# Cross attention with quantised operands: heads in the outer loop, two token tiles in the inner, values applied to 256 columns at once

## The chip, the cores and the metric

One core of one Trainium2 chip runs the whole kernel. The metric is the device time of one execution in microseconds (us), lower being better. TensorE (PE in the profile), VectorE (DVE), ScalarE (ACT) and GpSimd (POOL) each run their own list of instructions in order, and wait for one another on semaphores; SyncE (SP) issues the loads and stores.

## What is computed

A decoder of two layers over two sequences of 256 tokens (512 tokens of width 256): attention, cross attention and a feed-forward part in each layer, each followed by adding the input and a normalisation over the 256 features. The change lies in the cross attention of the second layer, cut here to what matters:

```python
q = (x @ Wq + bq).reshape(1, B * N, H, hd)
kv = (cond @ Wkv + bkv).reshape(1, -1, 2, H, hd)
...
q = _fq_sym(q, axis=-1)
k = _fq_sym(k, axis=-1)
v = _fq_sym(v, axis=2)
attn = jnp.einsum('bhqd,bhkd->bhqk', q, k)
attn = jax.nn.softmax(attn.astype(jnp.float32), axis=-1)
attn = _fq_unsigned(attn, axis=-1)
out = jnp.einsum('bhqk,bhkd->bhqd', attn, v)
out = jnp.transpose(out, (0, 2, 1, 3)).reshape(B, N, C)
return out @ Wp + bp
```

There are 16 heads of 16 features, 512 queries and 1024 keys. `_fq_sym` rounds to whole steps of the largest magnitude divided by 127, `_fq_unsigned` to 255 steps. The kernel takes exp(score - maximum + log 255) and converts it to int16, which is the rounded probability before the division by the sum.

## The kernel before, in words

The program is six stages, each ended by its residual addition and normalisation; stage 5 is the one above. Its 512 queries are four token tiles of 128 (TT = 4), and a **unit** is one head of one token tile: 64 units, numbered u = 16 i + h (tile i outside, head h inside). A unit passes over four engines:

- PE multiplies the queries of the unit with all keys, two products of 512 columns into two banks of PSUM (`scores`, line 927).
- DVE adds the zero, writes the scores to SBUF in `sx` and takes their maximum per row (`maximum`, line 1390; the profile calls it CUSTOM_DVE_ANT_0). POOL turns the maximum into a bias (line 442).
- ACT takes the exponential of `sx` into `px` as int16, with the sum of each row (line 562).
- PE turns the 1024 columns, eight transposes of 128 columns through `ident_b` (`turn`, line 936), into bank 4 or 5.
- DVE or ACT copies that bank to `pTx` and casts it (`evacuate`, line 1399, or `evac_px`, line 580). Which one is set by `SHARE`: of every seven units ACT takes numbers 1, 3 and 5 (27 of 64), DVE the other four (37).
- PE multiplies the turned probabilities with the values, eight products of 128 columns with 32 columns of weights (`apply`, line 947), into bank 6 or 7.

The order of the work is written out by hand. In step u PE issues scores(u + 3), turn(u), apply(u - 1). DVE issues maximum(u + 2) and evacuate(u). ACT issues exp(u) and evac_px(u - 1). Scores have two pairs of banks, `sx` and `px` three buffers each, `pTx` two.

Each token tile is closed while the units of the next one run: ACT takes the 256 columns of sums out of PSUM (`evac_sums`, line 589), DVE inverts the sums of rows (line 1403), PE turns them (`turn_z`, line 955), ACT copies them (line 595), PE spreads them over the features (`spread_z`, line 961), DVE multiplies (`normalise`, line 1408), PE projects (`project`, through the helper of line 630), DVE adds the residual (`add`, line 1413) and takes the statistics (lines 1130 and 1131), POOL the inverse deviation (lines 391 and 392), and DVE scales (line 1136). The fourth tile has no units behind it, so these steps run one after another at the stage's end. PE then transposes the result for stage 6 (line 690).

## Time and profile before

| | |
|---|---|
| time of three executions | 565.52 us median (565.0 to 566.82) |
| span of the profiled execution | 564.0 us, 7942 instructions; the three executions above have no span shown, and what lies around this span is not shown apart |
| PE | 501.8 us busy, 89% of the span |
| DVE | 347.0 us busy, 62% |
| ACT | 232.3 us busy, 41% |
| POOL | 111.9 us busy, 20% |
| stage 5, first maximum to last product | 329.8 to 441.9 us |
| chain of work that ended last | PE 71%, DVE 18%, ACT 5% |

The shares are means over six stages of different kinds. PE's busy time counts matmuls that overlap in the engine's pipeline, so it says little about how much room PE has; the starts of its instructions say more.

### The profile page before, as it was taken

The page shows a single profiled execution, that of the slowest core. Times are in us where ns is not written, and L with a number is a line of the kernel's source. Part 1 is how long each engine was busy: PE and PEld are TensorE (multiplying, and loading weights), DVE is VectorE, ACT ScalarE, POOL GpSimd, SP SyncE. Part 2 cuts the span into 40 slices and gives each one's busy share as a digit, 9 for nine tenths or more (in the row PEclk, how much of TensorE's full clock was granted, in tenths as well). Part 3 has the DMA queues.
Part 4 walks back from the last instruction along what each step waited for, and adds up shares of the span by engine and source line. Part 5 has one row for each costly group of instructions (what it writes and reads, how often), then busy time and mean ns, then how long its engine had stood idle before and what let it go on. Part 6 is the DMA issues. An engine that isn't in the chain of part 4 may idle for free.

```text
span 564.0 us, 7942 instructions
## 1 busy us (share of the span) xinstructions
PE 501.8 (89%) x2848; PEld 321.1 (57%) x2879; DVE 347.0 (62%) x845; ACT 232.3 (41%) x546; POOL 111.9 (20%) x209
## 2 busy tenths in 40 slices
PE   4696979999979999999997389999998788999994
PEld 2264556666645567776676246676666545455552
DVE  2996367454556766666654679999999373121224
ACT  3331321222223764445541169999898420010100
POOL 8695033232333000000002501111111000000002
PEclk9987988999988999999999759999999889999998
DMA  8900000000000000000000060000000400000001
GB/s 309 309 20 1 1 0 1 1 2 0 1 0 0 2 1 1 2 1 1 1 1 0 0 273 28 2 2 2 2 2 2 150 0 0 0 1 0 0 1 37
DMA packets 9671, 16.32 MB, mean 29 GB/s; under 512 B 1305, under 2 KB 8281, under 8 KB 9305
## 3 DMA queue, kind: packets, MB, share of 16 engines
q1 hardware_dynamic: 9632, 15.82, 8.4%
q8 instruction: 23, 0.38, 0.3%
q14 instruction: 16, 0.12, 0.1%
HBM read 15.29 MB, written 0.52 MB: 28 GB/s over the span
## 4 chain that ended last, share of the span: by engine, by line
PE 71%; DVE 18%; ACT 5%; issue 4%; DMA 1%; POOL 1%; SPq 0%; POOLq 0%; DVEq 0%; ACTq 0%
PE ps L630 16%; PE ps L848 8%; PE ps L816 8%; PE ps L1033 5%; PE ps L780 5%; PE ps L947 4%; PE ps L829 4%; PE ps L927 4%; PE ps L744 4%; PE ps L936 4%; PE ps L751 3%; ACT area_b L562 2%; DVE area_a L1390 2%; PE ps L721 1%; DVE stats L1130 1%
## 5 line engine op out<-in xcount | busy, mean ns | idle before, releaser
L1390 DVE CUSTOM_DVE_ANT_0 area_a<-ps,zero,small 128x1024 f32<-128x1024 f32 x64 | 80.0, 1272 | 1.3 <-PE ps L927 1.3
L562 ACT ACTIVATE area_b<-area_a,small 128x1024 int16<-128x1024 f32 x64 | 72.9, 1142 | 5.9 <-POOL small L442 5.7
L391 POOL TENSOR_SCALAR var_eps<-meanvar 128x1 f32<-128x1 f32 x24 | 6.0, 252 | 288.0 <-DVE meanvar L1131 287.5
L630 PE MATMUL ps<-xT_odd,area_a 128*128 128x512 f32 x128 | 59.4, 609 | 0.0
L816 PE MATMUL ps<-area_a,area_b 128*128 128x512 f32 x96 | 49.4, 625 | 0.3 <-DVE area_a L1267 0.2
L1472 DVE TENSOR_TENSOR area_b<-ps,area_b 128x512 f32<-128x512 f32 x16 | 11.0, 688 | 59.3 <-ACT area_b L606 59.3
L848 PE MATMUL ps<-area_b,area_a 128*32 128x128 f32 x384 | 47.4, 275 | 0.0
L606 ACT ACTIVATE area_b<-ps 128x512 f32<-128x512 f32 x16 | 9.6, 597 | 84.6 <-PE ps L630 84.6
L936 PEld LDWEIGHTS ps<-ident_b,area_b 128*128 128x128 bf16 x512 | 34.0, 99 | 17.4 <-ACT area_b L562 5.3
L927 PE MATMUL ps<-area_b 128*128 128x512 bf16 x107 | 35.8, 404 | 7.5 <-DVE small L1390 3.5
L848 PEld LDWEIGHTS ps<-area_b,area_a 128*32 128x32 f32 x384 | 39.1, 110 | 5.7 <-issue 5.3
L947 PE MATMUL ps<-area_a,area_b 128*32 128x128 bf16 x512 | 40.0, 221 | 1.0 <-ACT area_a L580 0.8
L936 PE MATMUL ps<-ident_b,area_b 128*128 128x128 bf16 x512 | 40.0, 222 | 0.8 <-ACT area_b L562 0.7
L543 ACT ACTIVATE area_a<-area_b,small 128x128 f32<-128x128 f32 (+1 forms) x64 | 28.3, 443 | 28.8 <-DVE small L1279 28.8
L543 ACT ACTIVATE area_a<-area_a,small 128x128 f32<-128x128 f32 (+1 forms) x64 | 28.3, 443 | 27.9 <-DVE small L1279 27.9
L630 PEld LDWEIGHTS ps<-xT_odd,area_a 128*128 128x128 f32 x128 | 25.1, 197 | 25.3 <-issue 24.6
L947 PEld LDWEIGHTS ps<-area_a,area_b 128*32 128x32 bf16 x512 | 28.9, 97 | 9.0 <-issue 1.7
L829 PEld LDWEIGHTS ps<-ident,area_a 128*128 128x128 f32 x192 | 22.7, 141 | 18.1 <-issue 14.3
L442 POOL TENSOR_SCALAR small<-small 128x1 f32<-128x1 f32 x64 | 12.4, 194 | 101.9 <-DVE small L1390 101.9
L1033 PE MATMUL ps<-area_a,area_b 128*128 128x256 f32 x128 | 31.6, 391 | 0.9 <-DVE area_b L1477 0.9
L1279 DVE CUSTOM_DVE_ANT_0 area_a<-ps,window 128x128 f32<-128x128 f32 (+1 forms) x64 | 19.1, 354 | 21.0 <-PE ps L816 21.0
L519 ACT ACTIVATE area_a<-ps 128x512 f32<-128x512 f32 x16 | 9.6, 597 | 53.6 <-PE ps L751 53.6
(259 smaller groups left out, 896.5 us busy)
## 6 DMA issues: line engine op xcount, KB each, us to landing
area_a<-in_w_up_dram SPq DMA_DIRECT2D x1, 4096.0 KB, 13.6
area_a<-in_w_down_dram SPq DMA_DIRECT2D x1, 2048.0 KB, 8.2
area_b<-in_idx_row_dram SPq DMA_DIRECT2D x1, 1024.0 KB, 7.2
ctxT<-in_ctxT_dram SPq DMA_DIRECT2D x1, 1024.0 KB, 9.2
ctx_tok<-in_ctx_dram SPq DMA_DIRECT2D x1, 1024.0 KB, 12.8
w_qkv<-in_w_qkv_dram SPq DMA_DIRECT2D x1, 768.0 KB, 5.9
xT_even<-in_xT_dram SPq DMA_DIRECT2D x1, 512.0 KB, 3.9
wkvx<-in_wkvx_dram SPq DMA_DIRECT2D x1, 512.0 KB, 10.0
```

Source lines behind the costliest of these rows:

```text
L543: a = act.activation(unit_p1(u)[:, j, 0:nk, :], s1[u % 2][:, j, 0:nk * P].rearrange("p (b k) -> p b k", b=nk), ACT.Exp, bias=nmx1[:, u % 2 ...
L562: act.activation(px[:, u % PX, :], sx[:, u % 3, :], ACT.Exp, bias=nbx[:, u:u + 1], accum_out=zx[:, i, h:h + 1]).then_inc(sem("px_ready"), 1)
L630: mm = pe.matmul(dst, lhsT(c), rhs(c), start=start and c == 0, stop=stop and c == DC - 1, **kw)
L780: mm = pe.matmul(proj(i), prod[:, j % 2, i * P:(i + 1) * P], row_hot[:, j, :], start=False, stop=j == SJ - 1, skip_group_check=True)
L816: mm = pe.matmul(dst, qT1[:, g8, i * P:(i + 1) * P], kT1[:, g8 // UC, :, kt * P:(kt + 1) * P], start=True, stop=True)
L829: mm = pe.transpose(bank(4, 2)[:, at:at + P], unit_p1(u)[:, j, b, :], ident[:])
L848: mm = pe.matmul(dst, v1[:, (kt * (H1 // HU) + g8) * HU + j, :], unit_pT1(u)[:, j, b, :], start=j == 0 and b == 0, stop=j == HU - 1 and b ...
L927: mm = pe.matmul(bank(2 * (u % 2) + half), qTx[:, h // 2, h % 2, i * P:(i + 1) * P], kTx[:, h // 2, half * 512:(half + 1) * 512], start=Tr ...
L936: mm = pe.transpose(bank(4 + u % 2).bitcast(BF16)[:, k * P:(k + 1) * P], px[:, u % PX, k * P:(k + 1) * P].bitcast(BF16), ident_b[:])
L947: mm = pe.matmul(dst, ivh[:, k * HX + h, :], pTx[:, u % 2, k * P:(k + 1) * P], start=h % 2 == 0 and k == 0, stop=h % 2 == 1 and k == KT - 1)
L1033: mm = pe.matmul(proj(i), hidden[:, g % 2, i * P:(i + 1) * P], w_down[:, g, :], start=g == 0 and i % 2 == 0, stop=g == NG - 1, skip_group_ ...
L1390: dve.tensor_tensor_reduce(sx[:, u % 3, :], bank(2 * (u % 2), 2), zero[:].broadcast_to([P, B * M]), qsc[:, u // HX, u % HX:u % HX + 1], LO ...
```

## The change

Units are numbered anew: u = 32 b + 2 h + t, where b is a half (two token tiles), h the head and t the tile in the half. Two neighbouring units share a head, and the values are applied to both in one product of 256 columns. Division, projection and the steps around them are done once per half, 256 tokens wide, of which the residual, the statistics and the scaling stay per tile. The `SHARE` table, the depth of all queues and the number of score, maximum, exponential and evacuation instructions stay. One of the two `pTx` buffers moves to another area, and each holds 8 pieces of 256 columns, so an evacuation writes 8 pieces of 128 columns at a distance of 256.

```diff
-        rzTx = sb("rzTx", [HX, P])
-        attTx = sb("attTx", [P, 2, DC, P])
+        rzTx = sb("rzTx", [HX, 2 * P])
+        attTx = sb("attTx", [P, DC, 2 * P])
...
-        pTx = carve("a", DC * E1 * 2 * HE + 3 * B * M, [2, KT * P], BF16)
+        pTx = [carve("a", DC * E1 * 2 * HE + 3 * B * M, [KT, 2 * P], BF16), carve("b", 26 * N, [KT, 2 * P], BF16)]
...
+        def unit5(u):
+
+            b, rest = divmod(u, 2 * HX)
+            return b, rest // 2, rest % 2
...
             def evac_px(u):
                 act.wait_ge(sem("pTx_ps"), u + 1)
-                if u >= 2:
-                    act.wait_ge(sem("ox_ps"), u - 1)
-
-                act.activation(pTx[:, u % 2, :], bank(4 + u % 2).bitcast(I16), ACT.Copy).then_inc(sem("pTx_act"), 1)
...
+                if u >= 4:
+                    act.wait_ge(sem("ox_ps"), u // 2 - 1)
+
+                act.activation(pTx[u // 2 % 2][:, :, u % 2 * P:(u % 2 + 1) * P], bank(4 + u % 2).bitcast(I16).rearrange("p (k q) -> p k q", q=P),
+                               ACT.Copy).then_inc(sem("pTx_act"), 1)
...
-                def apply(u):
-
-                    i, h = divmod(u, HX)
-                    pTx_ready(pe, u)
+                def apply(m):
+
+                    b, h, _ = unit5(2 * m)
+                    pTx_ready(pe, 2 * m)
+                    pTx_ready(pe, 2 * m + 1)
                     c, pair = divmod(h // 2, P // PAIR)
-                    dst = bank(6 + i % 2)[pair * PAIR:(pair + 1) * PAIR, c * P:(c + 1) * P]
+                    dst = bank(6 + b)[pair * PAIR:(pair + 1) * PAIR, 2 * c * P:2 * (c + 1) * P]
                     for k in range(KT):
-                        mm = pe.matmul(dst, ivh[:, k * HX + h, :], pTx[:, u % 2, k * P:(k + 1) * P],
+                        mm = pe.matmul(dst, ivh[:, k * HX + h, :], pTx[m % 2][:, k, :],
                                        start=h % 2 == 0 and k == 0, stop=h % 2 == 1 and k == KT - 1)
                     mm.then_inc(sem("ox_ps"), 1)
...
+                def project(b):
+                    pe.wait_ge(sem("attx_ready"), b + 1)
+                    for t in range(2):
+                        dense(bank(6 + b)[:, t * D:(t + 1) * D], lambda c: attTx[:, c, t * P:(t + 1) * P],
+                              lambda c: wpx[:, c, :]).then_inc(sem("proj5"), 1)
...
-                    if u > HX and u % HX == 3:
-                        turn_z(u // HX - 1)
-                    if u > HX and u % HX == 5:
-                        spread_z(u // HX - 1)
-                    if u > HX and u % HX == 7:
-                        project(u // HX - 1)
-                    if u % HX == 1 and u > 2 * HX:
-
-                        pe.wait_ge(sem("res5_ready"), u // HX - 1)
-                    if u:
-                        apply(u - 1)
-                turn_z(TT - 1)
-                spread_z(TT - 1)
-                project(TT - 1)
+                    if u == 2 * HX + 3:
+                        turn_z(0)
+                    if u == 2 * HX + 5:
+                        spread_z(0)
+                    if u == 2 * HX + 7:
+                        project(0)
+                    if u and u % 2 == 0:
+                        apply(u // 2 - 1)
+                turn_z(1)
+                spread_z(1)
+                project(1)
...
                 def add(i):
-                    dve.wait_ge(sem("proj5"), i + 1)
+                    dve.wait_ge(sem("proj5"), 2 * (i // 2) + 2)
...
-                invert_z(TT - 1)
-                normalise(TT - 1)
-                add(TT - 1)
-                norm_stats(5, TT - 1)
-                norm_scale(5, TT - 1)
+                    at = u - 2 * HX
+                    if at == 1:
+                        invert_z(0)
+                    if at == 6:
+                        normalise(0)
+                    if at in (8, 10):
+                        add(at // 2 - 4)
+                        norm_stats(5, at // 2 - 4)
+                    if at == NORM_AT:
+                        norm_scale(5, 0)
+                    if at == NORM_AT + 2:
+                        norm_scale(5, 1)
+                invert_z(1)
+                normalise(1)
+                for i in range(2, TT):
+                    add(i)
+                    norm_stats(5, i)
+                for i in range(2, TT):
+                    norm_scale(5, i)
```

Where the order moves, in three places. First PE between two steps of the plain stretch, before (line 927 is scores, 936 turn, 947 apply):

```order
L927 MATMUL ps<-area_b 128x512 x2
L936 MATMUL ps<-ident_b,area_b 128x128 x8
L947 MATMUL ps<-area_a,area_b 32x128 x8
L927 MATMUL ps<-area_b 128x512 x2
L936 MATMUL ps<-ident_b,area_b 128x128 x8
L947 MATMUL ps<-area_a,area_b 32x128 x8
```

And with the change (line 935 is scores, 944 turn, 956 apply):

```order
L935 MATMUL ps<-area_b 128x512 x2
L944 MATMUL ps<-ident_b,area_b 128x128 x8
L935 MATMUL ps<-area_b 128x512 x2
L944 MATMUL ps<-ident_b,area_b 128x128 x8
L956 MATMUL ps<-area_a,area_b 32x256 x8
```

The apply of odd steps is gone, and the one of even steps carries 256 columns in each of its eight products. Second PE at the end of the stage, before (line 630 is the projection first and stage 6's router and gate products last, 690 the transposes for stage 6):

```order
L947 MATMUL ps<-area_a,area_b 32x128 x16
L955 MATMUL ps<-ident,small 16x128
L961 MATMUL ps<-rzTx,pair_rows 128x128 x2
L630 MATMUL ps<-wpx,attTx 128x256 x2
L690 MATMUL ps<-ident,x_odd 128x128 x8
```

And with the change:

```order
L956 MATMUL ps<-area_b 32x256 x8
L965 MATMUL ps<-ident,small 16x128 x2
L972 MATMUL ps<-rzTx,pair_rows 128x256 x2
L637 MATMUL ps<-wpx,attTx 128x256 x4
L697 MATMUL ps<-ident,x_odd 128x128 x8
```

The steps are the same, but all of them are twice as wide or twice as many. Third DVE at the end of the stage, behind the last evacuation, before (line 1403 inverts, 1408 normalises, 1413 adds):

```order
L1403 RECIPROCAL small<-small 128x16
L1408 TENSOR_TENSOR attTx<-ps,attTx 128x256
L1413 TENSOR_TENSOR res<-ps,x_even 128x256
L1130 BN_STATS stats<-res 128x6
L1131 BN_AGGR meanvar<-stats 128x2
L1136 TENSOR_SCALAR x_odd<-res,meanvar,rstd 128x256
```

And with the change:

```order
L1415 RECIPROCAL small<-small 128x32
L1420 TENSOR_TENSOR attTx<-ps,attTx 128x512
L1425 TENSOR_TENSOR res<-ps,x_even 128x256
L1140 BN_STATS stats<-res 128x6
L1141 BN_AGGR meanvar<-stats 128x2
L1425 TENSOR_TENSOR res<-ps,x_even 128x256
L1140 BN_STATS stats<-res 128x6
L1141 BN_AGGR meanvar<-stats 128x2
L1146 TENSOR_SCALAR x_odd<-res,meanvar,rstd 128x256 x2
```

Two tiles now stand in the part of DVE's list that has no units behind it, where one stood; in the loop there are two tiles where three stood.

## Rows read from the trace of the kernel before

**Rows 1.** Chain of waits over 355.6 to 436.8 us, its shares by line.

```profile
by line: PE ps L947 17.8%; PE ps L927 16.7%; PE ps L936 16.3%; issue 12.5%; ACT area_b L562 12.2%; DVE area_a L1390 7.8%; ACT area_a L580 5.3%; PE ps L630 3.4%; DVE area_a L1399 2.5%; PE ps L961 2.4%; DVE small L1390 1.0%; ACT attTx L589 0.
```

**Rows 2.** Busy time by stretch: length, then PE, PEld, DVE, ACT, POOL, granted clock, DMA.

```profile
344.00:356.00 12.00, 11.45 (x136) 8.20 (x138) 12.00 (x22) 11.65 (x20) 1.52 (x8) 1.00 0.01 2
355.60:436.80 81.20, 75.69 (x861) 54.41 (x876) 78.89 (x141) 75.35 (x126) 11.50 (x53) 1.00 0.01 2
```

**Rows 3.** Timeline of DVE (start, duration, engine): the maxima of units 7, 8 and 14.

```profile
341.54 1.27 DVE L1390 CUSTOM_DVE_ANT_0 area_a<-ps,zero,small 128x1024 f32<-128x1024 f32 x1
342.74 1.28 DVE L1390 CUSTOM_DVE_ANT_0 area_a<-ps,zero,small 128x1024 f32<-128x1024 f32 x1
...
352.52 1.27 DVE L1390 CUSTOM_DVE_ANT_0 area_a<-ps,zero,small 128x1024 f32<-128x1024 f32 x1
```

**Rows 4.** Timeline of PE, one step of the loop without waits.

```profile
374.80 0.61 PE L927 MATMUL ps<-area_b 128*128 128x512 bf16 x2
375.24 0.61 PE L936 MATMUL ps<-ident_b,area_b 128*128 128x128 bf16 x8
375.78 0.62 PE L947 MATMUL ps<-area_a,area_b 128*32 128x128 bf16 x8
376.33 0.39 PE L927 MATMUL ps<-area_b 128*128 128x512 bf16 x1
```

**Rows 5.** Timeline of DVE around a residual: maxima 42 and 43, an evacuation before.

```profile
399.23 0.69 DVE L1399 CAST area_a<-ps 128x1024 bf16<-128x1024 int16 x1 [0.28 <-PE ps L936]
399.83 1.28 DVE L1390 CUSTOM_DVE_ANT_0 area_a<-ps,zero,small 128x1024 f32<-128x1024 f32 x1
...
402.07 1.28 DVE L1390 CUSTOM_DVE_ANT_0 area_a<-ps,zero,small 128x1024 f32<-128x1024 f32 x1
```

**Rows 6.** Groups by line: count, busy us, mean ns of one, idle before.

```profile
L1408 DVE TENSOR_TENSOR attTx<-ps,attTx 128x256 f32<-128x256 f32 x4 | 1.7, 420 | 2.7 <-PE ps L961 2.7
L1136 DVE TENSOR_SCALAR x_odd<-res,meanvar,rstd 128x256 f32<-128x256 f32 x3 | 1.2, 407 | 0.0
L1403 DVE RECIPROCAL small<-small 128x16 f32<-128x16 f32 x4 | 1.0, 247 | 0.0
L1472 DVE TENSOR_TENSOR area_b<-ps,area_b 128x512 f32<-128x512 f32 x16 | 11.0, 688 | 59.3 <-ACT area_b L606 59.3
L1327 DVE COPY area_b<-ps 128x512 bf16<-128x512 bf16 x4 | 1.4, 416 | 0.0
```

**Rows 7.** Timeline: what follows what across engines, units 9, 35 and 39.

```profile
344.61 1.27 DVE L1390 CUSTOM_DVE_ANT_0 area_a<-ps,zero,small 128x1024 f32<-128x1024 f32 x1
346.20 1.15 ACT L562 ACTIVATE area_b<-area_a,small 128x1024 int16<-128x1024 f32 x1 [0.35 <-POOL small L442]
...
389.48 1.02 ACT L580 ACTIVATE area_a<-ps 128x1024 bf16<-128x1024 int16 x1
390.39 1.15 ACT L562 ACTIVATE area_b<-area_a,small 128x1024 int16<-128x1024 f32 x1
391.69 0.62 PE L936 MATMUL ps<-ident_b,area_b 128*128 128x128 bf16 x8
...
398.58 0.61 PE L936 MATMUL ps<-ident_b,area_b 128*128 128x128 bf16 x8
```

**Rows 8.** Chain of waits at the end of stage 5 (start, us, what).

```profile
441.32 0.64 PE ps L947 x8
...
441.98 0.63 ACT attTx L589 x2
...
443.37 0.72 PE ps L961 x4
...
444.60 1.15 PE ps L630 x4
```

**Rows 9.** PE's clock: a stretch of the stage's end, and wide f32 products of stage 5's start.

```profile
445.80:449.00 3.20, 1.92 (x10) 1.15 (x8) 1.41 (x4) 1.15 (x3) 0.77 (x2) 0.50 1.10 356
...
309.48 3.77 PE L630 MATMUL ps<-wqx,xT_even 128*128 128x256 f32 x9 [0.56 <-ACT xT_even L491]
```

More of the change, by code:

```diff
@@ L443, in _ @@
                                            ALU.mult, ALU.add).then_inc(sem("biasx_ready"), 1)
-                        if u > HX and u % HX == NORM_AT - 1:
-                            inverse_deviation(5, u // HX - 1)
-                for i in range(TT - 1 if n == 5 else 0, TT):
+                        if u - 2 * HX == NORM_AT - 1:
+                            inverse_deviation(5, 0)
+                        if u - 2 * HX == NORM_AT + 1:
+                            inverse_deviation(5, 1)
+                for i in range(TT // 2 if n == 5 else 0, TT):
                     inverse_deviation(n, i)
@@ L562, in stage5 @@
                     act.activation(px[:, u % PX, :], sx[:, u % 3, :], ACT.Exp, bias=nbx[:, u:u + 1],
-                                   accum_out=zx[:, i, h:h + 1]).then_inc(sem("px_ready"), 1)
+                                   accum_out=zx[:, 2 * b + t, h:h + 1]).then_inc(sem("px_ready"), 1)
                     if u and by_scalar(u - 1):
                         evac_px(u - 1)
-                    if h == 1 and i:
-                        evac_sums(i - 1)
-                    if h == 4 and i:
-                        evac_z(i - 1)
+                    if u == 2 * HX + 1:
+                        evac_sums(0)
@@ L570, in stage5 @@
+                    if u == 2 * HX + 4:
+                        evac_z(0)
                 if by_scalar(TT * HX - 1):
                     evac_px(TT * HX - 1)
[L572 to L573 removed]
+                evac_sums(1)
+                evac_z(1)
             def evac_px(u):
                 act.wait_ge(sem("pTx_ps"), u + 1)
[L577 to L580 removed]
@@ L588, in evac_sums, with evac_z @@
                 for c in range(DC):
-                    a = act.activation(attTx[:, i % 2, c, :], bank(6 + i % 2)[:, c * P:(c + 1) * P], ACT.Copy,
-                                       scale=vsc[:, c:c + 1])
+                    a = act.activation(attTx[:, c, :], bank(6 + b)[:, 2 * c * P:2 * (c + 1) * P], ACT.Copy, scale=vsc[:, c:c + 1])
                 a.then_inc(sem("sumsx_out"), 1)
-            def evac_z(i):
-                act.wait_ge(sem("rzTx_ps"), i + 1)
-                act.activation(rzTx[:], bank(6 + i % 2)[0:HX, 0:P], ACT.Copy).then_inc(sem("rzTx_ready"), 1)
+            def evac_z(b):
+                act.wait_ge(sem("rzTx_ps"), b + 1)
+                act.activation(rzTx[:], bank(6 + b)[0:HX, 0:2 * P], ACT.Copy).then_inc(sem("rzTx_ready"), 1)
@@ L920, in scores @@
                 def scores(u):
-                    i, h = divmod(u, HX)
+                    b, h, t = unit5(u)
+                    i = 2 * b + t
                     if u >= 2:
@@ L957, in spread_z, with turn_z @@
-                def spread_z(i):
-                    pe.wait_ge(sem("rzTx_ready"), i + 1)
+                def turn_z(b):
+                    pe.wait_ge(sem("rzx_ready"), b + 1)
+                    pe.wait_ge(sem("sumsx_out"), b + 1)
+                    for t in range(2):
+                        mm = pe.transpose(bank(6 + b)[0:HX, t * P:(t + 1) * P], rzx[:, 2 * b + t, :], ident[:])
+                    mm.then_inc(sem("rzTx_ps"), 1)
+                def spread_z(b):
+                    pe.wait_ge(sem("rzTx_ready"), b + 1)
@@ L960, in spread_z @@
                     for c in range(DC):
-                        mm = pe.matmul(bank(6 + i % 2)[:, D + c * P:D + (c + 1) * P], pair_rows[:, c * P:(c + 1) * P], rzTx[:],
+                        mm = pe.matmul(bank(6 + b)[:, 2 * c * P:2 * (c + 1) * P], pair_rows[:, c * P:(c + 1) * P], rzTx[:],
                                        start=True, stop=True)
                     mm.then_inc(sem("zfx_ps"), 1)
-                def project(i):
-                    pe.wait_ge(sem("attx_ready"), i + 1)
-                    dense(bank(6 + i % 2)[:, 0:D], lambda c: attTx[:, i % 2, c, :], lambda c: wpx[:, c, :]).then_inc(sem("proj5"), 1)
+                def project(b):
+                    pe.wait_ge(sem("attx_ready"), b + 1)
+                    for t in range(2):
+                        dense(bank(6 + b)[:, t * D:(t + 1) * D], lambda c: attTx[:, c, t * P:(t + 1) * P],
+                              lambda c: wpx[:, c, :]).then_inc(sem("proj5"), 1)
```

56 lines of the change are left out of this document (21 added, 35 removed).

## The prediction

> **What bounds the kernel now.** I read the chain of waits first, then busy time by stretch, then the starts of single instructions. The chain over units 16 to 63 is half PE: apply, scores and turn have 51% of it between them [rows 1]. That invites the reading that fewer PE instructions shorten the loop. The busy times say something else: from 344 to 356 us DVE is busy for 12.00 of 12.00 us, and from 355.6 to 436.8 us for 78.89 of 81.20, against 75.35 of ACT and 75.69 of PE, whose time counts overlaps [rows 2]. The chain names PE because PE is nearly as late, not because it is the scarcest.
>
> The three rates, per unit:
> - DVE: the maxima of units 7 and 14 start 352.52 - 341.54 = 10.98 us apart, and one period of the seven-unit share table lies between them, so 1.57 us a unit with nothing else on DVE. Two maxima in a row start 1.20 apart, and one behind an evacuation another 0.60 later [rows 3, 5].
> - PE: scores to turn 0.44, turn to apply 0.54, apply to scores 0.55, together 1.53 [rows 4].
> - ACT: 1.14 for an exponential, and about 0.91 from an evacuation's start to the next exponential [rows 7]; 1.14 + 0.91 x 3/7 = 1.53.
>
> So three engines lie within 3%, and DVE is first. Closing a tile puts more on DVE: residual and statistics cost (402.07 - 399.83) - 1.20 = 1.04 [rows 5], normalising, scaling and inverting their durations less the 0.08 that neighbours overlap, 0.34, 0.33 and 0.17 [rows 6]. That is 1.88 a tile. From maximum 16 (355.6) to maximum 63 (436.8) that makes 47 x 1.57 + 3 x 1.88 = 79.3 us of 81.2: DVE waits only for the other 1.9.
>
> **The change part by part.**
>
> 1. *DVE's work in the loop.* Of three closings two stay, merged: inverting about 0.25, one normalisation of 512 columns 0.69 - 0.08 = 0.61 (from the 512-column product of stage 6 [rows 6]), twice 1.04, twice 0.33: 3.6 in place of 5.6. **-2.0.**
>
> 2. *PE's work in the loop.* Apply goes from 16 products of 128 columns to 8 of 256 for two units. The columns are the same, 2048. Two products of 512 take 0.44, so 256 columns should take about 0.11 and eight 0.88, with the change of weight width around 0.97. No row shows a 256-column bf16 product with 32 columns of weights; the 128-column one is the lower end (0.55 for eight) and the 512-column one the upper (1.76), and I take the straight line between them, since both lie on it. A pair of steps then takes 0.44 + 0.54 + 0.97 + 0.44 + 0.44 = 2.83 for 3.07: the last 0.44 assumes that turn to scores costs less where no switch to 32 columns lies between; otherwise 2.93. So PE comes down to 1.42 to 1.47 a unit. PE is not first, so this buys only DVE's waits, at most all 1.9. **-1.9.** Half the weight loads are gone too; they ran beside the products and cost nothing.
>
> 3. *PE's work comes in lumps.* Even steps now take 1.95 and odd ones 0.88, while DVE wants its turned bank every 1.57. Follow one maximum: 1.59 to its exponential (344.61 to 346.20), 1.30 to its turn (390.39 to 391.69), 0.54 to apply, 0.97 to the scores, 0.44 to the next turn, 0.65 to its evacuation (398.58 to 399.23), 0.60 to a maximum four units on [rows 4, 5, 7]. Sum 6.09, against 4 x 1.57 = 6.28 of DVE; before it was 5.67. It fits by 0.2, if the exponential starts at once. Where it stands behind an evacuation on ACT it starts up to 0.9 later, and then DVE waits. Bounds: nothing, or 0.22 (0.42 longer, 0.2 of it spare) at each of 24 pairs, 5.3. I take one wait of 0.3 to 0.4 per 14 units over the 48 units without a closing, 1.2, and 0.5 for the steps in which spread and a double projection stand between two turns on PE (1.3 more than for one tile, but DVE has its own closing work then). **+1.7.**
>
> 4. *The end of the stage.* This has no cover: each step waits for the one before [rows 8]. The last apply grows by 0.42; the two copies of sums by 0.1 each, as ACT's 1024 columns take 1.15; the turned sums and their copy by about 0.1 each, an estimate from half of what spread pays per product; spread (0.72) comes to what four products of 256 columns take (1.15), +0.43; normalising +0.27; the projection doubles, +0.86 (four more products of 0.216, read as the spacing in its 1.15 for four); DVE adds and measures one more tile before the last, +1.04. The scaling of the third tile lies under POOL's work for the fourth. Sum 0.42 + 0.2 + 0.2 + 0.43 + 0.27 + 0.86 + 1.04. **+3.4.** The router behind it waits for all of it.
>
> 5. *At nothing:* the evacuations. They now write 8 pieces of 128 columns. The bf16 copy of line 1327 writes pieces of 16 at a distance, and takes 416 ns for 512 elements, well under the 688 of a 512-element f32 product [rows 6]. Waiting for a free `pTx` is looser than before. The load of `w_down` still starts behind the last apply, and its user comes 20 us later.
>
> Sum: -2.0 - 1.9 + 1.7 + 3.4 = **+1.2 us**. Against the profiled span of 564.0 that is 565.2; the median of the runs shown lies 1.5 above that span, so 566.7 by the median's measure. A measurement of this kernel tells about 0.3%, 1.7 us, from no change.
>
> **A rule against it.** The trace shows one-tile pieces at the end of the stage finishing in turn, and the sum above charges 3.4 for doubling them. The Trainium skill, "Perfetto Trace Analysis", section "Optimizing Scalar/DVE Operations", says both that grouping into larger operations helps a saturated engine and that where an engine is not saturated but causes bubbles elsewhere, breaking instructions up may finish work sooner. DVE is the first in the loop and the second at the end; by the first half alone the merged normalisations would be all gain, 0.15 each, by the second the end pays.
>
> **The rivals.**
>
> - *PE sets the loop* (0.07). For it: the chain of waits [rows 1]. Then 32 pairs save 0.24 each, 7.7, and the loop's closings on PE shrink by about 2; with the end's 3.4 this is 6.3 faster, 559.2. Against it: DVE at 12.00 of 12.00.
> - *The lumps cost nothing* (0.14). Then -2.0 - 1.9 + 3.4 = -0.5, 565.0. For it: 0.2 to spare in the chain of four units.
> - *PE's clock falls before the last projection* (0.22), the case on the slower side. At 445.8 the granted clock falls to 0.50, that is 1.2 GHz for 2.4, after PE had only the short steps of the closing [rows 8, 9]. The projection was just over. Now it begins later behind a thinner stretch. Half clock costs 0.42 a product (3.77 for nine [rows 9]) in place of 0.216: eight products 1.6 more, the transposes 0.3. It decides if the clock falls before the projection starts: 566.7 + 1.9 = 568.6.
> - *The lumps cost all they can* (0.07): 5.3 for 1.7, 570.3.
> - *The cast loses its speed by writing in pieces* (0.03). As slow as the maximum's 1.27 for 0.69, 37 times: +21, 588. Line 1327's row speaks against it. The Trainium skill, "VectorE: DVE Perf Modes", section "Rules for kernel authors", ties the top rate to dense step-1 operands, by which a broken destination could mean this case; its section "What auto-detection actually checks" asks only for step 1 in 16-bit operands, and the row agrees with the latter.
>
> **How the numbers follow.** The forecast has 0.47. Its own uncertainty, 0.7 in the end's sum and 1 in the lumps, spreads it over 565.3 to 568, of which a sixth (0.08 of all) lies beyond 567.2, where slower by 0.3% begins. Faster by over 0.3% (under 563.8) is only the PE rival, 0.07. Slower: 0.08 + 0.22 + 0.07 + 0.03 = 0.40. The rest, 0.53, is within. The range from 564.6 to 569.6 takes in the clock and the case without lumps, and leaves out the PE rival, the worst lumps and the slow cast.
>
> **What would show it.** Right: maxima 7 to 14 still about 11 us apart, DVE near 98% of the loop, an apply of 0.9 to 1.0, a maximum 63 some 2 us earlier (434 to 435), and from the last apply's start to the projection's end 6.8 us in place of 4.4 (441.32 to 445.75 [rows 8]). Wrong: a seven-unit period under 10.9 (then DVE was not first) or over 11.4 (then the lumps bind); the projection's products spaced by 0.4 (the clock); evacuations above 0.75. The forecast fails most easily in the third part, which no row shows.

## The result and the profile after

Slower, and by more than the range allowed for.

| | before | after |
|---|---|---|
| median, runs on the same chip | 565.28 us (565.0 to 566.82) | 572.23 us (570.05 to 573.69) |
| ratio | 1 | 1.0113, 95% interval 1.0082 to 1.0145 |
| span of the profiled execution | 564.0 us | 571.9 us |
| mean granted clock in it | 0.944 | 0.936 |
| first maximum of stage 5 | 329.83 | 330.52 |
| maximum 63 | 436.80 | 438.46 |
| start of the last apply | 441.32 | 443.64 |
| router scores leave PE's bank (the activation behind stage 6's first products) | 452.34 | 460.23 |
| from there to the end | 111.7 | 111.7 |

The profiled execution of the change is the longest of its four (573.69; the others took 573.47, 570.99 and 570.05), so its span lies 7.9 above the one of before where the medians lie 6.9 apart. The positions in the lower rows are times within the profiled execution, in us.

Busy time by stretch, the columns as in [rows 2] (length, PE, PEld, DVE, ACT, POOL, clock, DMA):

```profile
344.00:356.00 12.00, 11.43 (x109) 7.51 (x108) 11.49 (x19) 11.90 (x19) 1.33 (x7) 1.00 0.01 2
355.60:438.00 82.40, 75.62 (x679) 49.28 (x677) 78.62 (x134) 74.65 (x119) 10.71 (x52) 0.98 0.01 1
406.40:409.80 3.40, 1.53 (x15) 0.78 (x13) 3.33 (x10) 2.15 (x3) 1.18 (x4) 1.00 0.01 2
409.80:413.20 3.40, 3.40 (x19) 2.05 (x18) 3.13 (x7) 2.48 (x4) 0.26 (x2) 0.50 0.00 0
441.00:447.30 6.30, 3.83 (x30) 2.63 (x30) 1.41 (x3) 2.30 (x5) 0.00 (x0) 1.00 0.20 49
447.30:464.30 17.00, 14.00 (x39) 9.28 (x38) 6.89 (x27) 4.48 (x7) 1.73 (x4) 0.50 0.32 107
```

DVE, which had not a hundredth to spare in the plain stretch [rows 2], is idle for 0.51 us in 12. And the clock falls twice: inside the loop at 409.8, where it had been 1.00 over the same units before, and at 447.3, where it stays at half until 464.3.

One and a half pairs of steps on PE, against [rows 4]:

```profile
402.15 0.61 PE L944 MATMUL ps<-ident_b,area_b 128*128 128x128 bf16 x8
402.69 1.05 PE L956 MATMUL ps<-area_b 128*32 128x256 bf16 x8
403.67 0.60 PE L935 MATMUL ps<-area_b 128*128 128x512 bf16 x2
404.11 0.61 PE L944 MATMUL ps<-ident_b,area_b 128*128 128x128 bf16 x8
404.56 0.59 PE L935 MATMUL ps<-area_b 128*128 128x512 bf16 x2
```

The apply takes 0.98 to the next product (402.69 to 403.67), turn to scores 0.45 where no apply lies between: the 0.97 and 0.44 of the prediction. The Trainium skill, "TensorE: Matmul & The Clock Gate", section "Wait — 56ns, not 53.3ns?", gives a warm product's distance as its columns at 2.4 GHz and about 2.5 ns. From that comes an estimate of 0.87 for eight products of 256 columns; the trace has 0.98, and the change to weights 32 columns wide can account for most of the rest, since turn to apply took 0.54 [rows 4] where turn to scores takes 0.45. The casts that write in pieces cost what they did, 691 ns:

```profile
L1410 DVE CAST area_b<-ps 128x1024 bf16<-128x1024 int16 x19 | 13.1, 691 | 4.9 <-PE ps L944 4.7
```

Maxima 14, 28, 32, 48 and 63 on DVE. The table of shares has a period of seven units, so 14 to 28 is two periods of the plain loop:

```profile
353.80 1.28 DVE L1401 CUSTOM_DVE_ANT_0 area_a<-ps,zero,small 128x1024 f32<-128x1024 f32 x1
...
376.41 1.27 DVE L1401 CUSTOM_DVE_ANT_0 area_a<-ps,zero,small 128x1024 f32<-128x1024 f32 x1
...
382.57 1.28 DVE L1401 CUSTOM_DVE_ANT_0 area_a<-ps,zero,small 128x1024 f32<-128x1024 f32 x1
...
413.72 1.28 DVE L1401 CUSTOM_DVE_ANT_0 area_a<-ps,zero,small 128x1024 f32<-128x1024 f32 x1 [0.21 <-PE ps L935]
...
438.46 1.27 DVE L1401 CUSTOM_DVE_ANT_0 area_a<-ps,zero,small 128x1024 f32<-128x1024 f32 x1
```

14 to 28 is 22.61, where two periods of before are 21.96 (2 x 10.98 [rows 3]). The waits between 353.8 and 376.4 (who, for whom: us, times, longest) have one of DVE's for a turned bank:

```profile
PE ps L935 <- DVE small L1401: 0.8, 2, 0.6
...
DVE area_a L1410 <- PE ps L944: 0.4, 1, 0.4
```

PE stands up to 0.6 us for DVE before the scores of a step, and later DVE stands for PE: the steps without an apply leave PE idle, those with the whole apply are too long to catch up in.

From 32 to 48 it is 31.15 with two tiles closed in it. What happens there, on PE and DVE:

```profile
405.60 1.03 PE L956 MATMUL ps<-area_a,area_b 128*32 128x256 bf16 x8
...
407.17 0.41 DVE L1425 TENSOR_TENSOR res<-ps,x_even 128x256 f32<-128x256 f32 x1
407.62 0.43 DVE L1140 BATCH_NORM_STATS2 stats<-res 128x6 f32<-128x256 f32 x1
...
408.20 1.28 DVE L1401 CUSTOM_DVE_ANT_0 area_a<-ps,zero,small 128x1024 f32<-128x1024 f32 x1
...
409.55 0.85 PE L935 MATMUL ps<-area_b 128*128 128x512 bf16 x2 [1.79 <-DVE small L1401]
...
411.19 1.89 PE L956 MATMUL ps<-area_b 128*32 128x256 bf16 x8
```

The second tile's addition and statistics come two units behind the first's, DVE falls back, PE stands for 1.79 us for the maximum at 408.20, and soon after it goes on the clock is at half: the same eight products take 1.89 for 1.03. (Whether the stand is what brought the clock down is a question for e4 below.)

The end of the stage, as the chain of waits has it, against [rows 8]:

```profile
443.64 1.05 PE ps L956 x8
...
444.71 0.85 ACT attTx L597 x2
...
445.69 0.39 PE ps L965 x2
...
446.11 0.38 ACT rzTx L602
...
446.54 1.35 PE ps L972 x4
...
447.91 0.70 DVE attTx L1420
...
448.65 3.80 PE ps L637 x8
...
452.47 0.44 DVE res L1425
...
456.88 3.32 PE ps L637 x16
```

The eight products of the projection take 3.80, where the four of before took 1.15 [rows 8]. The clock fell at 447.3, before them, and wide f32 products take 0.42 each at half clock [rows 9].

So the 7.9 us between the two spans are: 0.7 at the start of stage 5 (329.83 to 330.52, in code that the change doesn't touch; the runs below start it anywhere between 329.5 and 330.8); 1.0 from maximum 0 to maximum 63 (106.97 to 107.94), where 2.2 less had been forecast; 0.7 from there to the last apply (4.52 to 5.18); 5.6 from the last apply to the router's scores (11.02 to 16.59); nothing in stage 6.

### The profile page after: what moved, and what is told of

Read it like the earlier page. It is cut to its first block, busy times and chain, and to the rows that moved or that the text cites. A ratio compares the mean times of both kernels' runs of the same rounds, so it can differ in the third digit from the quotient of the medians.

```text
span 571.9 us, 7460 instructions
## 1 busy us (share of the span) xinstructions
PE 504.7 (88%) x2615; PEld 315.8 (55%) x2615; DVE 347.4 (61%) x841; ACT 232.1 (41%) x540; POOL 112.0 (20%) x209
## 4 chain that ended last, share of the span: by engine, by line
PE 67%; DVE 18%; ACT 7%; issue 5%; DMA 1%; POOL 1%; SPq 0%; POOLq 0%; DVEq 0%; ACTq 0%
PE ps L637 16%; PE ps L855 8%; PE ps L823 8%; PE ps L1043 5%; PE ps L787 5%; ACT area_b L569 4%; PE ps L751 4%; PE ps L836 4%; PE ps L758 3%; PE ps L935 3%; PE ps L956 3%; PE ps L944 2%; DVE area_a L1401 2%; PE ps L728 1%; DVE stats L1140 1%
## 5 line engine op out<-in xcount | busy, mean ns | idle before, releaser
L935 PE MATMUL ps<-area_b 128*128 128x512 bf16 x128 | 41.4, 409 | 6.4 <-DVE small L1401 5.1
L1043 PE MATMUL ps<-area_a,area_b 128*128 128x256 f32 x128 | 31.6, 391 | 0.9 <-DVE area_b L1493 0.9
L526 ACT ACTIVATE area_a<-ps 128x512 f32<-128x512 f32 x16 | 9.6, 597 | 54.5 <-PE ps L758 54.5
L1289 DVE CUSTOM_DVE_ANT_0 area_b<-ps,window 128x128 f32<-128x128 f32 (+1 forms) x64 | 19.0, 354 | 20.5 <-PE ps L823 20.5
L1300 DVE COPY area_b<-ps 128x512 f32<-128x512 f32 (+1 forms) x32 | 30.5, 953 | 1.6 <-PE ps L836 1.6
```

Source lines behind the costliest of these rows:

```text
L935: mm = pe.matmul(bank(2 * (u % 2) + half), qTx[:, h // 2, h % 2, i * P:(i + 1) * P], kTx[:, h // 2, half * 512:(half + 1) * 512], start=Tr ...
L1043: mm = pe.matmul(proj(i), hidden[:, g % 2, i * P:(i + 1) * P], w_down[:, g, :], start=g == 0 and i % 2 == 0, stop=g == NG - 1, skip_group_ ...
L1289: m = dve.tensor_tensor_reduce(s1[u % 2][:, j, 0:nk * P].rearrange("p (b k) -> p b k", b=nk), unit_s1(u)[:, 0:nk, j, :], window[:, 2 - nk: ...
L1300: dve.tensor_copy(unit_pT1(u)[:, :, 0:nk, :], src).then_inc(sem("pT1_ready"), 1)
```

## The experiments

Four questions: is the period of 22.61 the lumps, or the new numbering and the new buffers? Is it the width of the product or how it is bunched? What of the end is the clock, what work without cover? What does closing two tiles at one place cost? "A to scores" is the time from the start of the last apply to the router's scores; the columns before it are distances between maxima. All these and the span are from each run's profiled execution; the median is over all of a kernel's executions.

| kernel | 0 to 32 | 14 to 28 | 32 to 48 | 48 to 63 | A to scores | span | median | ratio, 95% interval |
|---|---|---|---|---|---|---|---|---|
| before | 53.1 | | 27.3 | 26.6 | 11.0 | 564.0 | 565.3 | |
| after | 52.1 | 22.61 | 31.2 | 24.7 | 16.6 | 571.9 | 572.2 | 1.0082 to 1.0145 |
| e1_single | 50.6 | 21.97 | 30.2 | 23.7 | 15.8 | 567.1 | 569.0 | 1.0034 to 1.0068 |
| e2_tile_order | 50.8 | 21.97 | 30.2 | 23.7 | 15.2 | 566.4 | 569.2 | 1.0041 to 1.0075 |
| e3_split | 50.1 | 21.88 | 31.6 | 23.7 | 15.9 | 568.5 | 570.1 | 1.0041 to 1.0096 |
| e4_warm_after | 51.7 | 22.60 | 30.5 | 24.1 | 12.8 | 567.5 | 568.9 | 1.0029 to 1.0063 |
| e5_warm_before | 52.9 | | 27.3 | 26.6 | 9.2 | 562.8 | 565.6 | 0.9984 to 1.0016 |
| e6_per_tile | 50.2 | 21.88 | 29.0 | 26.4 | 13.0 | 565.0 | 566.9 | 1.0018 to 1.0056 |
| e7_warm_both | 53.4 | | 27.3 | 26.6 | 9.2 | 562.8 | 564.7 | 0.9967 to 0.9987 |
| e8_tile_warm | 50.1 | 21.88 | 30.5 | 26.4 | 11.2 | 564.5 | 565.8 | 0.9982 to 1.0005 |
| e11_per_tile_only | 51.5 | 22.61 | 28.1 | 26.3 | 14.1 | 566.4 | 568.8 | 1.0038 to 1.0076 |
| e9_tile_warm_later | 50.1 | 21.88 | 27.6 | 26.3 | 11.2 | 561.3 | 563.1 | 0.9947 to 0.9972 |
| e12_tile_later | 50.2 | 21.88 | 27.6 | 26.4 | 15.1 | 567.3 | 567.8 | 1.0019 to 1.0042 |

(With before's order one tile is closed between 16 and 32, so 14 to 28 isn't the plain period there.)

Two things in this table mislead if they are read alone. Before closes one tile between maxima 32 and 48 and one between 48 and 63, so closing work is best compared over 32 to 63 as a whole: 53.9 before, 54.0 in e1, 53.9 in e9. And the column from 0 to 32 holds a stretch at half clock with which stage 5 starts in every run, and whose end moves between executions. The change and e11 run the same code there, with half clock up to 338.1 and 335.1:

```profile
337.00:338.00 1.00, 1.00 (x5) 0.45 (x6) 1.00 (x1) 1.00 (x2) 0.16 (x1) 0.50 1.14 492
```

```profile
336.00:337.00 1.00, 1.00 (x11) 0.66 (x12) 1.00 (x1) 1.00 (x2) 0.16 (x1) 1.00 0.68 295
```

Maxima 0 to 7 are 11.71 apart after the change and 11.16 in e11 (11.71 before, 11.17 in e9, 12.02 in e7), while 7 to 32 takes 40.34 in both. So a difference of up to 0.9 in that column need not be the edit's.

### The apply of one unit again, in the new order

```diff
-                def apply(m):
+                def apply(u):
...
-                        mm = pe.matmul(dst, ivh[:, k * HX + h, :], pTx[m % 2][:, k, :],
+                        mm = pe.matmul(dst, ivh[:, k * HX + h, :], pTx[u // 2 % 2][:, k, u % 2 * P:(u % 2 + 1) * P],
...
-                    if u and u % 2 == 0:
-                        apply(u // 2 - 1)
+                    if u:
+                        apply(u - 1)
```

> The changed kernel with the values applied per unit again (eight products of 128 columns after each turn); heads outside and the closing per half stay. Before takes 565.3 us, the change 572.2. If the lumps that a product for two units makes on PE cost time (theory lumps), the distance of maximum 14 to maximum 28 falls from 22.6 back to 22.0 us and the time by 1.5 to 3, to about 570. The rival, that the 256 columns bought something and all the loss sits in the closing, has PE back at 1.53 us a unit and the time at 573 to 575. The stage's end, last apply to the router's scores, is 15.9 to 16.6 us in either (11.0 before).

The sums of a head's two tiles are started in turn in one bank here, and the result is off by 6%: part of the first tile's sum is probably not kept. All instructions are there, and the next run has the same loop without this fault. The period is that of before again. Maxima 14 and 28, 21.97 apart:

```profile
352.93 1.27 DVE L1400 CUSTOM_DVE_ANT_0 area_a<-ps,zero,small 128x1024 f32<-128x1024 f32 x1
...
374.90 1.27 DVE L1400 CUSTOM_DVE_ANT_0 area_a<-ps,zero,small 128x1024 f32<-128x1024 f32 x1
```

The casts into pieces, the moved buffer and the merged closings are all still in this kernel, so none of them is the 0.65. From 32 to 48 it still takes 30.2 for before's 27.3, at full clock all through, and the end hardly changes: they are not the lumps. But from 32 to 63 it takes 54.0 for before's 53.9, so closing both tiles at one place costs the loop nothing there. And from 7 to 63 it takes 93.0, with eight products of 128 columns for each unit on PE as before; the fastest kernel below, e9, takes 92.8 with the wide ones. What the wide products save PE is worth at most 0.2 us in the loop.

### The old numbering inside a half as well

```diff
-            return b, rest // 2, rest % 2
+            return b, rest % HX, rest // HX
```

> As the run with the values per unit, and the tiles outside the heads again: of the change only the closing per half is left. If the order of heads and tiles has no price of its own, this takes the same as that run within 1 us, about 570, so the closing per half alone costs 4 to 5 us against before (565.3). The rival, that heads outside cost or gain something through waits, has the two apart by more than 1.7 us.

The loop is that of the run above to 0.2 us, and the end 0.6 shorter: which unit stands beside which costs nothing.

### The wide apply, half of it in each step

```diff
-                def apply(m):
+                def apply(m, part):
...
-                    for k in range(KT):
+                    for k in range(part * KT // 2, (part + 1) * KT // 2):
...
-                    if u and u % 2 == 0:
-                        apply(u // 2 - 1)
+                    if u >= 2:
+                        apply(u // 2 - 1, u % 2)
```

> The changed kernel with the eight 256-column products of a pair issued four after one turn and four after the next, so PE's steps are even at about 1.4 us and every product stays. Theory lumps: maximum 14 to maximum 28 takes 22.0 us for 22.6, the time falls by 2 to 3, to 569 to 570. Rival: the unevenness costs nothing, the distance stays at 22.6 and the time at 572.

With four products of 256 columns in each step the period is 21.88. DVE is busy all the time again; the same stretch of 24 us here and after the change:

```profile
354.00:378.00 24.00, 23.04 (x211) 14.15 (x213) 24.00 (x42) 23.63 (x40) 3.05 (x16) 1.00 0.01 2
```

```profile
354.00:378.00 24.00, 22.63 (x212) 14.70 (x210) 23.43 (x39) 23.14 (x37) 2.86 (x15) 1.00 0.01 2
```

Width is harmless, bunching costs 0.64 (against e1) to 0.73 per 14 units. But the half-apply of the first half's last pair now comes a step later, and ACT, at its old place in the list, stood 1.31 us for it: 31.6 from 32 to 48. That is this experiment's own fault, and e9 and e12 mend it.

### Extra products that keep PE at work through the end, after and before

```diff
+            def warm(k):
+                for _ in range(k):
+                    pe.matmul(bank(2), ident_b[:], kTx[:, 0, 0:512], start=True, stop=True)
...
+                warm(4)
                 turn_z(1)
+                warm(1)
                 spread_z(1)
+                warm(3)
                 project(1)
```

Nobody reads their bank; five and two more stand before the transposes of the last two tiles. The kernel before gets the same in e5 (3, 1, 2 and 4 of them).

> The changed kernel with 15 extra bf16 products of 512 columns into a bank that nobody reads, in the gaps that PE has between the steps of the last closing. Theory clock: PE's granted clock stays at 1.00 there, the projection's eight products take 2.1 us for 3.8, spread 1.2 for 1.35, the sixteen router products 1.8 for 3.3, and the time falls by 3 to 4, to about 568.7. Rival: the clock falls anyway, or what it costs lies beside other waits: 572 or, with the extra products in the way, 573. The loop before maximum 63 stays as it is.

> The kernel before with 10 extra bf16 products of 512 columns in PE's gaps at the stage's end (bank unread). The run that did so on the changed kernel cut last apply to router scores by 3.8 us, but its stage 6 took 1.8 longer (113.5 for 111.65), since the clock fell at 463 us instead, just ahead of the gates' products. Theory give-back: here the sixteen router products gain 1.5, stage 6 loses about 1.8, and the time stays at 565 to 566. Rival: stage 6 loses nothing and the time is 563.8.

The projection and the router's second group of products in the chain of e4:

```profile
446.02 2.01 PE ps L637 x8
...
452.21 0.84 PE ps L637 x8
```

2.01 for 3.80, and 16.6 becomes 12.8. The kernel before gains as well in e5, 11.0 to 9.2, since the sixteen products of its router had taken 3.32 from 449.00 on, in the stretch of half clock that begins at 445.8 [rows 9], and take 1.75 now. So at full clock on both sides the longer end costs 12.8 - 9.2 = 3.6, and the clock adds 3.8 to one and 1.8 to the other.

Half of the gain is given back. The wide f32 product of stage 6 after the change and in e4:

```profile
471.71 1.98 PE L637 MATMUL ps<-xT_odd,w_su 128*128 128x512 f32 x4 [0.68 <-ACT area_b L618]
```

```profile
465.95 3.78 PE L637 MATMUL ps<-xT_odd,w_su 128*128 128x512 f32 x4 [0.68 <-ACT area_b L618]
```

After the change the clock had already fallen and recovered by then; in e4 it falls later, at 463.0, ahead of this product, which takes 1.8 more. In e5 the profiled execution gives 1.0 of 1.8 back, and the median is that of before, ratio 1.0000.

The end and stage 6 together thus gain 2.0 in e4, but its span is 4.4 below the change's (567.5 to 571.9) and its median 3.4 (568.86 to 572.23). The rest is an earlier start of stage 5 (0.7) and 1.7 in the loop, 0.4 of it in the first seven units. The loop had been expected to stay as it is: the code up to maximum 63 is the same, and the clock doesn't fall in it. PE stands just as long at the same place, with full clock before and behind:

```profile
404.70:408.10 3.40, 1.67 (x17) 1.15 (x16) 3.33 (x7) 2.45 (x5) 0.94 (x3) 1.00 0.01 2
408.10:411.50 3.40, 3.01 (x28) 1.98 (x28) 3.40 (x7) 2.48 (x4) 0.50 (x3) 1.00 0.00 0
```

```profile
408.47 0.60 PE L941 MATMUL ps<-area_b 128*128 128x512 bf16 x2 [1.79 <-DVE small L1410]
```

So the stand of 1.79 us was followed by a fall in one execution of this loop and not in another. What the fall costs is the difference of the two from 32 to 63, 55.9 to 54.5, about 1.3 us; what decides that it comes is not shown.

### Division and projection per tile, with the split apply

```diff
-                spread_z(1)
-                project(1)
+                spread_z(2)
+                spread_z(3)
+                project(2)
+                project(3)
...
-                normalise(1)
+                normalise(2)
+                normalise(3)
...
+                    if at == 14:
+                        normalise(1)
+                    if at in (8, 16):
+                        add(at // 8 - 1)
+                        norm_stats(5, at // 8 - 1)
```

The last tile uses bank 0, so that its products need not wait for those who read the third's. Sums and their turning stay per half; the first half's second tile is spread, projected and added eight units behind the first.

> The changed kernel with the pair's products split over two turns as before, and spread, normalising, projection and residual per tile instead of per half: in the loop eight steps apart, at the end one tile behind the other. Theory closing in one place: maxima 32 to 48 take 28.7 to 29.5 us for 31.1 (31.6 in the run with the split alone), the clock does not fall there, last apply to router scores takes 14 to 14.5 for 15.9, and the time is 566 to 567.5 for 570.1 (split alone). Rival: DVE's work is the same wherever it stands, so maxima 32 to 48 stay above 30 and the time above 569.

A to scores falls from 15.9 in e3 to 13.0: PE projects the third tile while DVE normalises the fourth, and DVE adds the third while PE projects the fourth. The Trainium skill, "Perfetto Trace Analysis", section "Optimizing Scalar/DVE Operations", says that where an engine is not saturated but makes others wait, breaking instructions up may finish work sooner. By it the end should be shorter; the traces agree. How much of the 2.9 us is the splitting takes other runs to tell, since here the clock falls only at 449.3, behind the projection: at full clock on both sides it is 1.6 (12.8 in e4, 11.2 in e8 below), and e12 below, which has this end too, takes 15.1 with an early fall. In the middle ACT stands for the sums as in e3:

```profile
386.43 0.84 ACT L601 ACTIVATE attTx<-ps,small 128x256 f32<-128x256 f32 x2 [1.31 <-PE ps L961]
```

### Extra products in stage 6 too

```diff
+                for _ in range(8):
+                    pe.matmul(bank(4), spread[:, 0:P], spread[:, 0:512], start=True, stop=True)
                 pe.wait_ge(sem("picked_ready"), TT)
...
+                for _ in range(2):
+                    pe.matmul(bank(4), spread[:, 0:P], spread[:, 0:512], start=True, stop=True)
                 pe.wait_ge(sem("gate1_ready"), 1)
```

and two more before the product with `w_su`; e7 is this on top of e5, e8 on top of e6 with extra products at the end (12 for e4's 15).

> The kernel before with the 10 extra products at the stage's end and 12 more in PE's gaps of stage 6's routing, on both sides of the gates' products. If the give-back in stage 6 is only the clock, stage 6 takes at most 111.7 us from the router's scores to the end, last apply to scores 9.5 for 11.0, and the time is 563.5 to 564.3. Rival: the extra products stand in the way or the clock falls all the same: 565 to 566.

> The run per tile, with extra products at the stage's end and in stage 6 as well. Last apply to router scores 11.5 or less, stage 6 at most 111.7: the time 563 to 564.5, that is, with its costs taken away one by one the change ends within 0.3% of before, and no lower. Rival: something of the change's cost is in none of these places, and the time stays at 566 or above.

Stage 6 is back at 111.65 in both. e7 has full clock from the last apply to the router's scores and beyond, and is the kernel before made 0.23% faster (interval 0.13 to 0.33%); its 564.7 is a little above what was expected. e8 missed its forecast of 563 to 564.5. In e8 the end is 11.2, but the clock fell in the middle of the loop, behind ACT's wait for the sums:

```profile
386.00:390.10 4.10, 2.20 (x19) 0.99 (x16) 2.62 (x7) 3.81 (x7) 0.38 (x2) 1.00 0.01 2
390.10:393.50 3.40, 3.40 (x18) 1.77 (x17) 2.65 (x5) 2.83 (x7) 0.21 (x2) 0.51 0.00 0
```

which is the picture of 406.4 and 409.8 above behind another wait: PE busy 2.20 of 4.10, then half clock, 30.5 for e6's 29.0. Again there is an execution of the same loop without the fall, that of e6, at the same place:

```profile
386.14:390.24 4.10, 2.20 (x19) 0.99 (x16) 2.62 (x7) 3.81 (x7) 0.38 (x2) 1.00 0.01 2
390.24:393.64 3.40, 3.40 (x32) 2.00 (x31) 3.25 (x6) 3.40 (x8) 0.38 (x2) 1.00 0.00 0
```

### Per tile alone, and per tile with everything and the sums a step later

e11 is the per-tile part of e6 on the change as it was, apply in one lump. e9 is e8 with one line:

```diff
-                    if u == 2 * HX + 1:
+                    if u == 2 * HX + 2:
                         evac_sums(0)
```

> The changed kernel with spread, normalising, projection and residual per tile (eight steps apart in the loop, one behind the other at the end), and the pair's eight products together again as in the change. Against the run per tile with split products (566.9) this puts the lumps back. Theory lumps and closing are separate: maxima 14 to 28 take 22.6 us, 32 to 48 29.5 to 30, last apply to router scores 13 to 13.5, time 568.5 to 569.5. Rival: with the closings apart the lumps are hidden, and the time stays at 567.

> The run per tile with split products and extra products at the stage's end and in stage 6 (565.8), with ACT's copy of the first half's sums one step later in ACT's list. In that run ACT stood 1.3 us at this copy for the last products of the half, and a clock drop at 390 us followed. Theory: the wait goes, maxima 32 to 48 take 28.5 for 30.5 and the time falls to 563.5 to 564.5, level with the kernel before with extra products (564.7). Rival: the copy holds ACT anyway, no change, 565.8.

e11 has the lumps' period (22.61) and no fall of the clock in the loop; with the second tile's closing moved eight units on, PE's longest stand is 1.06 for 1.79, and 32 to 48 takes 28.1 (29.5 to 30 had been expected). Of that, though, closing work has only moved: 32 to 63 is 54.4 in e11 and 30.5 + 24.1 = 54.5 in e4, which closes both at one place at full clock. So closing together costs the loop next to nothing while the clock holds, as e1 had it. The end takes 14.1 for the 13 to 13.5 expected: the clock falls at 444.3, before the projections.

e9 is the fastest of all, ratio 0.9960, and beats both kernels; against e8 it has no wait of ACT (1.4 of the 2.9 between 30.5 and 27.6) and no fall of the clock (the other 1.5). Its closing of the first half, and its end:

```profile
379.57:407.17 27.60, 26.65 (x236) 16.59 (x236) 26.80 (x50) 25.93 (x43) 3.94 (x18) 1.00 0.01 2
438.36:449.60 11.24, 10.20 (x63) 7.17 (x64) 3.79 (x11) 3.94 (x9) 1.71 (x4) 1.00 0.60 188
```

From maximum 0 to 63 it takes 104.0 (329.52 to 433.51), 3.0 less than before, of which 0.5 lies in the first seven units. Against e7, which has the same help for the clock, it is 1.5 ahead in span (562.8 to 561.3). But 0.6 of that is an earlier start of stage 5 and 0.9 the first seven units (12.02 to 11.17), and neither is the change's. What is: 2.4 less from maximum 7 to 63 (95.25 to 92.82), 0.3 more up to the last apply, 2.0 more at the end, together about 0.1. The medians are 1.6 apart, but from different chips, and the intervals of their ratios to before meet (0.9967 to 0.9987 and 0.9947 to 0.9972). So with every loss taken away the idea of the change is about even, and no gain over e7 is shown.

### The same without extra products

> The closing per tile with the split apply, the first half's sums copied one step later, and no extra products. If ACT's wait for the sums was what the closing of the first half still cost, maxima 32 to 48 lie 27.6 us apart as in the run with extra products (29.0 with the sums at their old step), and maximum 63 starts at 433.5. Then the end takes 13.0 us from the last apply to the router's scores, because PE's clock still falls before the transposes, and the span is 433.5 + 4.85 + 13.05 + 111.65 = 563.0, a median near 564.9, ratio 0.999. The rival is that the extra products gave the gain by keeping the clock in stage 5's last steps and in stage 6: then the middle is at 29 to 30 us again and the ratio stays at 1.003.

The edit is e6 with the line above. Its own forecast (span 563.0) was right on the middle of the loop and wrong behind it:

```profile
380.69:408.28 27.59, 25.93 (x232) 16.58 (x236) 26.79 (x48) 25.92 (x43) 3.96 (x18) 1.00 0.01 2
439.47:442.80 3.33, 1.81 (x13) 1.22 (x14) 0.15 (x1) 1.21 (x3) 0.00 (x0) 1.00 0.29 51
442.80:456.40 13.60, 12.49 (x42) 9.60 (x42) 5.02 (x22) 4.49 (x7) 1.63 (x4) 0.50 0.43 143
```

27.59 between maxima 32 and 48 as in e9, so that gain is the sums' place and not the extra products. But the clock fell at 442.8, 3.3 us behind the last apply's start, where in e6 it fell 9.0 behind it: both projections run at half clock (3.73 for eight in its chain) and the end takes 15.1 for 13.0. Stage 5 also starts 1.0 later than assumed, and stage 6 takes 1.1 longer, with another stretch of half clock from 466.7 to 470.1. The profiled execution is the longest of eleven. Its eleven runs spread from 566.69 to 569.12, at mean clocks of 0.950 to 0.935. The kernel of e9 spread over 1.6 us (563.02 to 564.62) at 0.954 to 0.961.

## Why the prediction was wrong

The median was forecast at 566.7 and is 572.2. By the prediction's own steps, against the span's +7.9 where +1.2 was forecast:

- **DVE bounds the loop; DVE's work -2.0.** Right. With e1 and e3 the period is back at DVE's own (21.97, 21.88), and from maximum 7 to 63 e1 takes 2.3 less than before, e9 2.4.
- **PE's relief removes DVE's waits, -1.9.** This step failed, by about 1.5 us. Over maxima 32 to 63 before and e9 both close two tiles, and take 53.9 each: no wait has gone. From 7 to 63 before had 1.8 of waits (95.26, less 56 x 1.5686 = 87.84 and 5.64 for three closings); e9, with 3.6 of closings, has 1.4 (92.82 - 87.84 - 3.6), 0.4 less. And e1, in which PE has no relief at all, is within 0.2 of e9. So the waits lay around the closings and came from them; with one closing fewer some went, and PE's pace per pair didn't take the others away. The step took a sum of waits for a reserve that one engine's speed would free. (Its sum for 16 to 63 is 79.4 rather than 79.3, so it had 1.8 and not 1.9 to give.)
- **Lumps, +1.7.** The mechanism was right and its size too small: one wait per 14 units as said (maxima 7 to 14 and 21 to 28 are 11.57 apart, over the 11.4 that was to mean that the lumps bind, 14 to 21 only 11.04), but 0.65 for the 0.3 to 0.4 assumed. After the change against e9, the loop has 1.5 more from maximum 7 to 32 and, with the clock's share left out, 0.6 behind it: 2.1 for 1.7. The sum of the chain of four units had 0.2 to spare only for a unit whose exponential starts at once, and PE's own stand before a step's scores, 0.6 in the row of waits, wasn't in it.
- **No fall of the clock in the loop** was assumed without being said. In the profiled execution it fell at 409.8, behind a stand of 1.79 us, and cost 1.3. I had charged the steps of the double closing 0.5 and asked whether DVE would wait, not whether PE would, and what could become of its clock. The stand is shown to belong to this loop, by e4; that it brings the clock down is not, since in e4 it didn't.
- **Maximum 63 to the last apply, 0.7,** had no term. The last but one apply, of 256 columns, stands on PE between the last exponential and its turn.
- **The end, +3.4.** Right at full clock: e4 less e5 gives 3.6. And right in its pieces, from the start of each to the start of the next: apply +0.41 for 0.42, sums +0.21 for 0.2, turned sums and copy +0.23 for 0.2, normalising +0.26 for 0.27, additions up to the router's first product +1.18 for 1.04. Spread grew by 0.62 for 0.43 and the projection by 2.65 for 0.86. This is the second step that failed: the end came to +5.6 because the projection was priced at full clock.
- **The rival of the clock (0.22)** is what happened to those two. Its condition, a fall before the projection starts, was met at 447.3; its price of 1.9 is near what e4 and e5 give, 3.8 less 1.8. The row that priced it was already in the prediction: by the prediction's own terms the projection would begin 1.5 us later behind the last apply (1.7 in the trace), and the fall had missed the old projection by less than 0.1 us (445.75 against 445.8). The chance given to it should have been the larger one.
- **The cast's rival and PE's rival** fell: 691 ns a cast, and no period under DVE's own.

Terms together: 1.2 forecast, 0.7 at stage 5's start, 1.5 + 0.4 + 1.3 in the loop, 0.7 to the last apply, 2.2 at the end: 8.0 with the rounding, of 7.9. The 0.7 at the start and the 1.3 of the clock in the loop are of this one execution, and the median, 1.0 lower, need not hold them in full.

What stays open: what decides when the clock falls. Behind the last apply's start it falls after 3.0 to 4.5 us in before, after the change, e1, e2, e3, e11 and e12, and after 9.0 in e6, whose code at that place is e12's. The table has a single profile of each kernel, and the columns on the end hold for that one: e6's profile is near its shortest execution (566.81 of 566.48 to 570.94), e12's is its longest.

## What to carry to other kernels

A product twice as wide at half the rate is free in work and not in time: where the queues between the engines are two or three deep, issue it in halves, one a step, and the others see the old beat. Steps that end a tile and have nothing to run beside them should stay as small as the tile even when the work before them is merged (1.6 us at full clock here), and what has no cover is to be counted together with PE's clock, since a longer thin stretch can put the next wide products on the far side of a fall that they had just escaped. Before a wait of the fullest engine is counted as time that another engine's relief will give back, look for what the wait stands beside: here it stood beside the closings, and stayed.

## What the hardware showed that I had not expected

- The clock can fall inside a loop in which PE is busy for 92% of the time: PE had stood 1.79 us in one place (1.53 busy of 3.40), and its products then ran at 0.50 from 409.8 to 413.2. The same loop with the same stand kept 1.00 in e4, and e6 and e8 are a second such pair (2.20 busy of 4.10 in both, then 1.00 and 0.51).
- Keeping the clock up at one place lets it fall at a later one. Of the 3.8 us that e4 won before the router 1.8 were lost again on the product with `w_su` (3.78 for 1.98), and only extra products in both places kept stage 6 at its 111.7.
- Executions of one kernel differ by several us, the longest at the lowest mean clocks: e12's eleven spread by 2.4, the three longest (569.10 to 569.12) at 0.935 and 0.936, and e6's ten by 4.5, the longest (570.94) at 0.936 where its shortest had 0.949.
